# Megakernel of two gated attention/FFN layers: the output projection of the first attention in f16 high and low parts, with the orders of three engines moved around it

## The chip, the cores and the metric

The kernel runs on one core of a Trainium2 chip. The metric is device time in microseconds (us) of one execution. The engines of the core are called by their short names: PE (TensorE, matmuls), DVE (VectorE), ACT (ScalarE), POOL (GpSimd) and SP (SyncE, which here only issues DMAs). Each engine works through its own instruction stream in order; semaphores join the streams.

## The reference

The input x has 16 batches of 128 tokens with 256 features. Four sub-layers follow each other, each added to x with a gate:

```python
x = x + tanh(g_xattn[0]) * xattn0(layernorm(x), ctx, boxes, ...)   # changed here
x = x + tanh(g_ffn[0])   * bitlinear_ffn(layernorm(x), ...)
x = x + tanh(g_xattn[1]) * xattn1(layernorm(x), ctx, ...)
x = x + tanh(g_ffn[1])   * mixture_of_experts(layernorm(x), ...)

# xattn0: 16 heads of 64, 128 queries and 128 keys in each batch
q, k, v = queries @ Wq.T + bq, keys @ Wk.T + bk, values @ Wv.T + bv
a   = einsum('bhqd,bhkd->bhqk', q, k) / 8
g   = relu(sin/cos features of box differences @ Wg + bg)
mn  = softmax(log(clip(g, 1e-6)) + a)
out = einsum('bhqk,bhkd->bqhd', mn, v).reshape(b, nq, 1024)
return out @ Wo.T + bo        # 1024 -> 256, the projection that changes
```

## The kernel before, in words

Only the first attention is touched. It is a loop over the 16 batches, written out for the first and the last ones, in which every engine has a function `iteration` with a fixed order of calls. Iteration b works on three batches at once: it makes scores, gates and probabilities of batch b, projects q, k and v of batch b+1, finishes batch b-1 (probabilities times values, transposition, output projection, residual), and normalises and transposes x of batch b+2. `has_x` is false in iterations 14 and 15, `has_q` in 15, and `has_c` (or `c`) in 0.

Matmul operands that must be exact to about f32 are kept as two f16 numbers, a high part (ACT makes it with a Copy) and a low part (the f32 value less the high part, made by DVE or POOL). A product then takes three passes, written `PAIRS`: high times high, high times low, low times high. Weights are scaled by `WSC` = 64 before the split and the scale is taken out when PSUM is read. The output projection is the exception: `OT` (the transposed attention output) and `WoT` are f32, and `project_o` makes eight f32 matmuls into bank 7.

What each engine does in an iteration, in order, as far as it is spoken of below:

- PE: `row_scores` 0 (L1706), `project_qk` of r = 0, 1 (L1678), `row_scores` 1 (waits for DVE's first two `row_max`), `project_qk` of r = 2, 3, `pv` (L1766, waits for POOL's low parts of the probabilities), `project_v` 0 (L1689), `turn_o` (L1780), `project_v` 1, `turn_xn` (L1655), `project_o` (L1786), `scores` 0 (L1721, L1728), gate 0 (L1743, L1747), `scores` 1 (waits until ACT has emptied banks 0 and 1), gates 1 to 3.
- ACT: `probs_high` (L1419), `ctx_high`, `qk_high` (L1406), the two box-feature steps Abs and Ln (L1351, L1355), `v_high` 0, `take_o` (L1377, `OT` from PSUM), `v_high` 1 (L1411), `xn_high` (L1370), a one-element Exp that loads its table early (L1452), two thirds of a negation of expert weights (`half_negated`, L1383), exps 0 and 1 (`EX`, L1393), the last third, exps 2 and 3, `feature_sine` (table load and Sin L1362, Copy L1366).
- DVE: `norm` (L862), `row_max` 0, 1 (L873), `take_qk` 0, 1, `row_max` 2, 3, `take_qk` 2, 3 (L894), `take_pv` (L882, L886), `feature_floor` (L846), `take_v` (L903), `feature_turns` (L851), `xn_low` (L867), `residual` (L909, L912, waits for `project_o`), `feature_fractions` (L855, L857), `feature_distance` (eight L839), `probs` (eight L923), `bn_stats` (L1012).
- POOL: issue of an accumulating weight DMA (`half_low`, L573), `probs_low` (L560), `feature_low` (L555), `split_qk` (L546), issue of another weight DMA (`half_high`, L569), `split_v` (L551), `split_ctx` (L516), and in iterations 0 to 6 `separable`, five small operations that build tables (L521 to L530).

The expert-weight work on ACT, POOL and SP has nothing to do with the attention; it is done here for the last sub-layer.

## Time and profile before

| what | value |
|---|---|
| median of 3 runs | 1169.16 us (1166.68 to 1172.12) |
| the profiled execution: time | 1164.61 us |
| its span, first to last instruction | 1162.8 us |
| mean granted TensorE clock over the span | 0.925 |
| busy: PE, DVE, ACT, POOL | 82%, 72%, 59%, 62% |
| first attention's probabilities of batch 0 begin at | 90.69 us |
| its last residual at | 485.7 us |
| `project_o`, f32 matmuls, all 16 batches | 64.5 us |

The first attention takes about 455 us of the 1163 us span; the rest belongs to the other three sub-layers. The page's share of busy time is an average over all of them, and the order and waits inside one iteration have to be read from the timeline and from the chain of waits. The projection's row on the page counts two matmul records for each f32 matmul.

### The profile page before, as it was taken

To read this page: it belongs to the slowest core of one execution; us is meant where nothing else is said; L and a number is where in the kernel's file an instruction comes from. 1 tells how busy PE (TensorE), PEld (TensorE's weight loads), DVE (VectorE), ACT (ScalarE), POOL (GpSimd) and SP (SyncE) were. 2 spreads that over 40 slices of the span, in tenths; PEclk is the share of its full clock that TensorE was granted. 3 is DMA by queue.
4 is the path that set the end of the run, shared out by engine and by line. 5 is a ranking of instruction groups with operands and counts; after the bars stand their busy time and mean duration, and the time that the engine had idled before them with its cause. 6 is when DMAs were issued, how large, how long until landed. Compare 5 with 4: busy or idle time off the path is not lost.

```text
span 1162.8 us, 32870 instructions
## 1 busy us (share of the span) xinstructions
PE 955.3 (82%) x12178; PEld 779.8 (67%) x12178; DVE 836.2 (72%) x1947; ACT 689.7 (59%) x1338; POOL 718.9 (62%) x811
## 2 busy tenths in 40 slices
PE   0448988899999996387878559995599999999996
PEld 0336766667777764364554248873599999999995
DVE  3997888877887775657776779985566666666663
ACT  2456878888888884145425548884354545454542
POOL 2988778886677752115341539984566766666663
PEclk9888999999999997669999869995799999999998
DMA  9276667678776756330001000000555215841251
GB/s 277 72 192 142 122 129 146 150 167 183 140 149 154 154 105 148 98 130 1 1 14 41 19 2 16 26 21 19 201 142 140 32 32 140 246 142 32 32 144 16
DMA packets 52118, 119.65 MB, mean 103 GB/s; under 512 B 7617, under 2 KB 30145, under 8 KB 51633
## 3 DMA queue, kind: packets, MB, share of 16 engines
q0 software_dynamic: 14144, 35.48, 21.3%
q1 hardware_dynamic: 35520, 80.71, 20.7%
q10 hardware_dynamic: 2352, 2.10, 0.6%
q8 instruction: 66, 1.08, 0.4%
q14 instruction: 36, 0.29, 0.1%
HBM read 212.54 MB, written 37.85 MB: 215 GB/s over the span
## 4 chain that ended last, share of the span: by engine, by line
PE 51%; DVE 18%; POOL 14%; ACT 6%; issue 5%; DMA 4%; POOLq 0%; ACTq 0%; SPq 0%; DVEq 0%
PE bank L2107 17%; PE bank L2121 9%; POOL PT L560 6%; PE bank L1786 6%; PE bank L1689 3%; PE bank L1766 2%; DVE nmx L1177 2%; ACT EX L1393 2%; PE bank L1728 2%; DVE h L1063 2%; PE bank L1937 2%; PE bank L1721 1%; DVE PT L923 1%; PE bank L1780 1%; DMA gates<-in_g_ffn 1%
## 5 line engine op out<-in xcount | busy, mean ns | idle before, releaser
L1623 ACT ACTIVATE yg<-bank,bms 128x128 f32<-128x128 f32 x312 | 107.8, 364 | 106.8 <-PE bank L2107 98.9
L1296 DVE TENSOR_TENSOR hm<-hf,hm 128x256 f16<-128x256 f32 x156 | 70.3, 450 | 81.5 <-ACT hm L1630 81.5
L1291 DVE SCALAR_TENSOR_TENSOR hf<-bank,bms,yg 128x128 f32<-128x128 f32 x312 | 98.1, 345 | 33.2 <-ACT yg L1623 32.0
L2107 PE MATMUL bank<-xT,wm_even 128*128 128x128 f16 x1920 | 115.6, 221 | 1.0 <-DVE xT L1303 1.0
L2107 PEld LDWEIGHTS bank<-xT,wm_even 128*128 128x128 f16 x1920 | 111.5, 99 | 2.1 <-DVE xT L1303 1.4
L560 POOL TENSOR_TENSOR PT<-PT 128x512 f16<-128x512 f32 x64 | 72.7, 1183 | 61.4 <-ACT PT L1419 61.4
L707 POOL DMA_INDIRECT out_x<-ys,sidx x39 | 62.8, 1611 | 76.2 <-DVE ys L1310 76.2
L2107 PE MATMUL bank<-xT,wm_odd 128*128 128x128 f16 x1824 | 108.0, 219 | 1.8 <-DMA wm_odd<-expert_weights 1.8
L2107 PEld LDWEIGHTS bank<-xT,wm_odd 128*128 128x128 f16 x1824 | 104.2, 98 | 2.4 <-issue 1.9
L1630 ACT ACTIVATE hm<-hf 128x256 f16<-128x256 f32 x156 | 64.5, 414 | 63.1 <-DVE hf L1291 61.7
L619 POOL TENSOR_TENSOR h<-h 128x512 f16<-128x512 f32 x32 | 40.6, 1281 | 83.0 <-DVE h L1063 81.0
L546 POOL TENSOR_TENSOR q<-qt,q 128x512 f16<-128x512 f32 x64 | 80.0, 1299 | 0.8 <-ACT q L1406 0.7
L666 POOL TENSOR_TENSOR P<-P 128x512 f16<-128x512 f32 x64 | 72.9, 1171 | 11.4 <-ACT P L1579 11.4
L1786 PE MATMUL bank<-WoT,OT 128*128 128x256 f32 x256 | 64.5, 409 | 1.9 <-ACT OT L1377 1.9
L700 POOL DMA_INDIRECT xin<-expert_tokens,gidx x39 | 42.0, 1076 | 31.1 <-POOL b2r L722 25.5
L1786 PEld LDWEIGHTS bank<-WoT,OT 128*128 128x128 f32 x256 | 50.9, 204 | 13.3 <-ACT OT L1377 6.1
L1406 ACT ACTIVATE q<-qt 128x512 f16<-128x512 f32 x64 | 38.8, 625 | 33.8 <-DVE qt L894 33.8
L2121 PE MATMUL bank<-wm_even,hm 128*128 128x256 f16 x480 | 55.7, 273 | 2.0 <-DVE hm L1296 2.0
L717 POOL TENSOR_SCALAR gts<-xin,etf 128x1 f32<-128x1 f32 x78 | 56.3, 1091 | 0.7 <-DMA xin<-expert_tokens,gidx 0.6
L1766 PE MATMUL bank<-vv,PT 128*128 128x65 f16 x768 | 33.9, 200 | 26.4 <-POOL PT L560 15.6
L1747 PE MATMUL bank<-We,F16s 128*128 128x256 f16 x384 | 53.7, 276 | 0.0
L1689 PE MATMUL bank<-wqkv,ctx 128*128 128x512 f16 x192 | 48.1, 390 | 6.4 <-DVE qt L894 6.4
(308 smaller groups left out, 2646.7 us busy)
## 6 DMA issues: line engine op xcount, KB each, us to landing
wm_even<-expert_weights SPq DMA_DIRECT2D x60, 1024.0 KB
wm_odd<-expert_weights SPq DMA_DIRECT2D x57, 1024.0 KB
expert_weights<-in_wcat POOLq DMA_DIRECT2D x16, 768.0 KB, 7.8
wsp<-expert_weights SPq DMA_DIRECT2D x16, 768.0 KB, 4.4
wsp<-in_wcat POOLq DMA_DIRECT2D x16, 768.0 KB, 10.3
expert_weights<-wsp SPq DMA_DIRECT2D x16, 768.0 KB, 3.3
Lst<-gate_tables SPq DMA_DIRECT2D x48, 68.0 KB, 6.0
gate_tables<-Lw SPq DMA_DIRECT2D x6, 512.0 KB, 3.3
```

Source lines behind the costliest of these rows:

```text
L546: nc.gpsimd.tensor_tensor(q16[:, par, w, 1, HS * g:HS * g + HS, :], qt[:, r, :, :], hi, ALU.subtract).then_inc(s_ql, 1)
L560: nc.gpsimd.tensor_tensor(PT16[:, 1, HS * g:HS * g + HS, :], PT[:, HS * g:HS * g + HS, :], PT16[:, 0, HS * g:HS * g + HS, :], ALU.subtract ...
L666: nc.gpsimd.tensor_tensor(P116[:, b % 2, 1, HS * g:HS * g + HS, :], P1[:, b % 2, HS * g:HS * g + HS, :], P116[:, b % 2, 0, HS * g:HS * g + ...
L707: nc.gpsimd.indirect_dma_start(out=a["out"], out_offset=bass.IndirectOffsetOnAxis(ap=sidx[:, t:t + 1], axis=0), in_=ys[:, t % 2, :], in_of ...
L1291: v.scalar_tensor_tensor(hf[:, (c // 2) % 2, c % 2, :], bank[c % 4][:, MT:2 * MT], bms[:, par, FC + c:FC + c + 1], yg[:, c % 4, :], ALU.ad ...
L1296: v.tensor_tensor(hm16[:, par, 1, c - 1:c + 1, :], hf[:, q % 2, :, :], hm16[:, par, 0, c - 1:c + 1, :], ALU.subtract).then_inc(m_hl, 1)
L1623: s.activation(yg[:, c % 4, :], bank[c % 4][:, 0:MT], ACT.Gelu, bias=bms[:, par, c:c + 1]).then_inc(m_g, 1)
L1630: s.activation(hm16[:, par, 0, 2 * q:2 * q + 2, :], hf[:, q % 2, :, :], ACT.Copy).then_inc(m_hh, 1)
L1689: ins = t.matmul(bank[2 + r][:, :], ctx16[:, par, xp, kk, :], wqkv16[:, 2, wp, kk, 512 * r:512 * r + 512], start=(n == 0), stop=(n == 5))
L1786: ins = t.matmul(bank[7][:, 0:D], OT[:, ch, :], WoT[:, ch, :], start=(ch == 0), stop=(ch == CH - 1))
L2107: ins = t.matmul(bank[c % 4][:, w * MT:(w + 1) * MT], wm16[par][:, wp, col:col + P], xT16[:, par, xp * KD + kk, :], start=(n == 0), stop=( ...
L2121: ins = t.matmul(bank[5 + par][:, 0:D], hm16[:, par, xp, c, :], wm16[par][:, wp, col:col + D], start=(n == 0), stop=(n == 3 * FC - 1))
```

## The change

The projection's operands become f16 pairs, `project_o` makes 24 f16 matmuls where it made eight f32 ones, and calls are moved in the `iteration` of PE, ACT and DVE:

- Weights: `WoT` goes; the f32 weights are loaded to the place that later holds `O` and the transposed output (8 KB of a partition), ACT makes `Wo16` high once behind the first `v_high`, and DVE makes `Wo16` low in iteration 0, just before `probs` of batch 0.
- ACT: `take_o` writes f16. `xn_high` moves behind exps 0 and 1, and all three thirds of the negation stand together between `xn_high` and exps 2 and 3.
- DVE: a new `o_low` (two operations of 128x512, f16 out) stands behind `take_v`. `residual` moves from before `feature_fractions` to behind `probs`. The private semaphore of the reciprocal is replaced by the common one.
- PE: `scores` 0 moves ahead of `turn_xn` and `project_o`; behind these come `scores` 1 and then all four gates. `turn_xn` also waits for the first `o_low`, `project_o` for both.

```diff
+            def o_low(c):
+                for r in range(2):
+                    dv.wait_ge(s_oc, 2 * c + r + 1)
+                    v.tensor_tensor(OT16[:, 1, 4 * r:4 * r + 4, :], bank[6 + r][:, :].rearrange("p (c n) -> p c n", c=4),
+                                    OT16[:, 0, 4 * r:4 * r + 4, :], ALU.subtract).then_inc(s_ol, 1)
...
                 dv.wait_ge(s_op, c + 1)
-                v.tensor_tensor(otmp[:, :], bank[7][:, 0:D], bo[:, :], ALU.add).then_inc(s_opt, 1)
+                v.scalar_tensor_tensor(otmp[:, :], bank[7][:, 0:D], 1.0 / WSC, bo[:, :], ALU.mult, ALU.add).then_inc(s_opt, 1)
...
                     take_v(b + 1)
+                if has_c:
+                    o_low(b - 1)
+                if has_q:
                     feature_turns(b + 1, 1 - par)
                 if has_x:
                     xn_low(b + 2, par)
-                if has_c:
-                    residual(b - 1)
-                    dv.wait_ge(s_xu, b)
...
+                if not has_c:
+                    dv.wait_ge(s_whi, 4)
+                    v.scalar_tensor_tensor(Wo16[:, 1, :, :], woT, WSC, Wo16[:, 0, :, :], ALU.mult, ALU.subtract).then_inc(s_wlo, 1)
+                    dv.wait_ge(s_wlo, 4)
                 probs(b, not has_c)
                 if has_c:
+                    residual(b - 1)
+                    dv.wait_ge(s_xu, b)
                     v.bn_stats(...)
...
+            ac.wait_ge(s_o, 64)
+            s.activation(Wo16[:, 0, :, :], woT, ACT.Copy, scale=WSC).then_inc(s_whi, 1)
...
                 if has_q:
                     v_high(b + 1, 1 - par, (1,))
+                if has_q:
+                    s.activation(warm[:, :], nmx[:, 0:1], ACT.Exp, scale=0.0)
+                exps(b, par, (0, 1), c == 0)
                 if has_x:
                     xn_high(b + 2, par)
-                if has_q:
-                    s.activation(warm[:, :], nmx[:, 0:1], ACT.Exp, scale=0.0)
-                exps(b, par, c == 0)
+                half_negated(b, par, range(NSP))
+                exps(b, par, (2, 3), c == 0)
...
             def project_o(c):
                 pe.wait_ge(s_oc, 2 * c + 2)
-                for ch in range(CH):
-                    ins = t.matmul(bank[7][:, 0:D], OT[:, ch, :], WoT[:, ch, :], start=(ch == 0), stop=(ch == CH - 1))
+                pe.wait_ge(s_ol, 2 * c + 2)
+                n = 0
+                for (wp, op) in PAIRS:
+                    for ch in range(CH):
+                        ins = t.matmul(bank[7][:, 0:D], OT16[:, op, ch, :], Wo16[:, wp, ch, :], start=(n == 0), stop=(n == 3 * CH - 1))
+                        n += 1
...
+                scores(b, par, 0)
                 if has_x:
                     turn_xn(b + 2, (None if c == 0 else 2 * b - 1))
+                if c == 1:
+                    pe.wait_ge(s_wlo, 4)
                 if c:
                     project_o(b - 1)
-                scores(b, par, 0)
+                scores(b, par, 1)
                 gate(b, par, 0, c == 0, has_q)
-                scores(b, par, 1)
                 gate(b, par, 1, c == 0, has_q)
```

## Rows read from the trace of the kernel before

**Rows 1.** Chain of waits, early iteration (start us, us, what).

```profile
229.50 0.56 PE bank L1766 x12
...
244.52 2.12 DVE fu L839 x8
...
254.59 0.55 PE bank L1766 x12
```

**Rows 2.** Chain of waits, one late iteration.

```profile
372.62 0.56 PE bank L1766 x12
...
378.97 3.70 PE bank L1786 x16
...
391.66 4.51 POOL PT L560 x4
396.22 0.55 PE bank L1766 x12
```

**Rows 3.** Timeline, late iteration (start us, us, engine, line, tiles, [idle before]).

```profile
374.62 4.96 POOL L546 TENSOR_TENSOR q<-qt,q 128x512 f16<-128x512 f32 x4
375.59 0.73 DVE L846 TENSOR_SCALAR fu<-fu 128x1024 f32<-128x1024 f32 x1
379.21 0.63 ACT L1411 ACTIVATE vv<-vf 128x512 f16<-128x512 f32 x1 [0.31 <-DVE vf L903]
380.15 0.42 DVE L867 TENSOR_TENSOR xn<-bank,xn 128x256 f16<-128x256 f32 x1
381.54 1.99 ACT L1383 ACTIVATE wsp<-wsp 128x1024 f16<-128x1024 f16 x2
382.71 0.42 DVE L909 TENSOR_TENSOR otmp<-bank,bo 128x256 f32<-128x256 f32 x1 [2.14 <-PE bank L1786]
383.18 0.49 DVE L912 SCALAR_TENSOR_TENSOR X<-otmp,tg,X 128x256 f32<-128x256 f32 x1
383.93 1.08 ACT L1393 ACTIVATE EX<-bank 128x512 f32<-128x512 f32 x2 [0.41 <-PE bank L1728]
386.50 1.09 ACT L1393 ACTIVATE EX<-bank 128x512 f32<-128x512 f32 x2 [0.54 <-PE bank L1728]
387.68 2.74 DVE L923 SCALAR_TENSOR_TENSOR PT<-bank,EX 128x256 f32<-128x256 f32 x8
```

**Rows 4.** Timeline, early iteration.

```profile
241.45 1.10 DVE L855 TENSOR_SCALAR fks<-fu 128x1024 f32<-128x1024 f32 x1
...
249.85 1.28 DVE L873 TENSOR_REDUCE nmx<-bank 128x4 f16<-128x512 f32 x2
...
251.61 2.85 PE L1678 MATMUL bank<-ctx,wqkv 128*128 128x128 f16 x48
```

**Rows 5.** Timeline, three DVE operations beside POOL operations.

```profile
67.84 1.23 DVE L862 TENSOR_SCALAR xn<-X,mv,rstd 128x256 f32<-128x256 f32 x1
...
103.49 4.05 DVE L846 TENSOR_SCALAR fu<-fu 128x1024 f32<-128x1024 f32 x1
...
464.58 1.24 DVE L967 TENSOR_SCALAR wqkv<-wqkv,thr 128x256 f32<-128x256 f32 x1
```

**Rows 6.** Timeline, operations like the added ones.

```profile
50.03 2.28 DVE L826 SCALAR_TENSOR_TENSOR wqkv<-wst,wqkv 128x2048 f16<-128x2048 f32 x1
...
384.05 0.83 PE L1747 MATMUL bank<-We,F16s 128*128 128x256 f16 x6
...
512.09 0.69 DVE L1054 TENSOR_TENSOR xg<-bank,xg 128x512 f16<-128x512 f32 x1 [0.54 <-ACT xg L1481]
```

**Rows 7.** Iteration 0: timeline, then chain of waits.

```profile
90.69 2.07 DVE L923 SCALAR_TENSOR_TENSOR PT<-bank,EX 128x256 f32<-128x256 f32 x6
...
95.94 4.53 POOL PT L560 x4
```

**Rows 8.** Windows (us, busy of PE, PEld, DVE, ACT, POOL, then granted clock, DMA).

```profile
129.12:254.59 125.47, 113.31 (x1450) 86.16 (x1451) 103.48 (x216) 102.35 (x145) 103.90 (x96) 1.00 0.70 147
...
437.10:439.20 2.10, 0.03 (x2) 0.00 (x0) 2.03 (x5) 2.07 (x5) 0.35 (x1) 0.91 1.02 126
```

More of the change, by code:

```diff
@@ L124, in build @@
         We16 = sb("We16", [P, 2, H * NN], F16, l0)
-        WoT = sb("WoT", [P, CH, D], F32, l0)
+        Wo16 = sb("Wo16", [P, 2, CH, D], F16, l0)
         bqk = sb("bqk", [P, 2, CH], F32, l0)
@@ L881, in take_pv @@
                         dv.wait_ge(s_oe, 4 * c + f - 1)
-                    v.reciprocal(rden[:, f % 2, :].unsqueeze(2), ps[:, :, DK:DK + 1]).then_inc(s_rd, 1)
-                    dv.wait_ge(s_rd, 4 * c + f + 1)
+                    step(v.reciprocal(rden[:, f % 2, :].unsqueeze(2), ps[:, :, DK:DK + 1]))
                     if f == 0 and not first:
@@ L1022, in _ @@
             take_pv(B - 1)
+            o_low(B - 1)
             residual(B - 1)
@@ L1376, in take_o @@
                         ac.wait_ge(s_op, c)
-                    s.activation(OT[:, 4 * r:4 * r + 4, :], bank[6 + r][:, :].rearrange("p (c n) -> p c n", c=4), ACT.Copy).then_inc(s_oc, 1)
+                    s.activation(OT16[:, 0, 4 * r:4 * r + 4, :], bank[6 + r][:, :].rearrange("p (c n) -> p c n", c=4), ACT.Copy).then_inc(s_oc, 1)
             def half_negated(h, par, qs):
@@ L1383, in half_negated, with exps @@
                     s.activation(wsp[:, par, c0:c1], wsp[:, par, c0:c1], ACT.Copy, scale=-1.0).then_inc(w_ng, 1)
-            def exps(b, par, first):
-                half_negated(b, par, range(NSP - 1))
-                for g in range(4):
-                    if g == 2:
-                        half_negated(b, par, (NSP - 1,))
+            def exps(b, par, gs, first):
+                for g in gs:
                     ac.wait_ge(s_st, 4 * b + g + 1)
```

14 lines of the change are left out of this document (9 added, 5 removed).

## The prediction

> **What bounds the kernel now.** I read the chain of waits first, since only a link of it can be worth time, and looked for what repeats. In every iteration of the first attention the chain passes from `pv` (L1766) over PE and DVE to the transposed output, through `project_o`, `scores` and exps to the probabilities, then through ACT's and POOL's split of them to the next `pv`. An iteration is the distance of two `pv` starts. While POOL builds the tables (early, five full iterations) it is 254.59 - 229.50 = 25.09 us, and the last link before the probabilities is DVE's `feature_distance` [rows 1]. Later (seven iterations) it is 396.22 - 372.62 = 23.60 us, and the last link is ACT: from exps 2 and 3 at 386.50 over sine to POOL's first `probs_low` at 391.66 is 5.16 us [rows 2, 3]. `project_o`, 3.7 us, lies on both chains. From here a time with a plus is counted from the start of `pv`.
>
> **Projection, scores, exps.** Six f16 matmuls of 256 columns take 0.83 us, of which 0.27 is the length of one, so 0.11 each; 24 take 2.8 against 3.7 us [rows 2, 6]. The saving of 0.9 hardly matters, because `scores` 0 now stands ahead of it, and exps 0 and 1 no longer wait for it. ACT becomes what they wait for: `v_high` 1 ends at +7.22 (379.84), the table load and the one-element Exp take 1.39 (from 380.15, where `xn_high` has ended, to 381.54), so exps 0 and 1 begin at +8.6 instead of +11.31 [rows 3]. Then `xn_high` ends at +10.0, three thirds of the negation (two take 1.99) fill ACT to +12.75, and exps 2 and 3 start there instead of at +13.88. PE is ready: `o_low` costs 2 x 0.69 and ends at about +8, `project_o` at +10.8, `scores` 1 at +12.1, gate 3, an estimate with the gates' own spacing, at about +16.3 [rows 3, 6]. `o_low` itself costs nothing here: DVE then has `feature_turns` (about 1 us) and still waits, because `xn_low` needs `xn_high`. That is what is late next: `xn_low` at +10.0 where it stood at +7.5, a loss of 2.5 us of DVE order that eats most of the gain from taking the residual out.
>
> **Late iterations.** `xn_low` (0.40) leads to `feature_fractions` at +10.4. From there to `probs` it was 383.67 (end of L912) to 387.68, 4.0 us, so `probs` begins at +14.4 instead of +15.06 [rows 3]. Behind it `bn_stats`, `norm` and `row_max` followed, `row_max` 3.3 us after the start of `probs` (249.85 less 246.6) [rows 1, 4]. Now the residual stands in between: 383.67 - 382.71 = 0.96, with the step to the next operation 0.99 us. Nothing hides it: `row_scores` 1, `project_qk` r = 2, 3 and `pv` are queued on PE behind `row_max`. And `norm`, an operation on SBUF alone, now falls at +18.4, after POOL's first `probs_low`, which starts at 12.75 + 5.16 = +17.9 (it used to fall ahead of it). The same operation beside a POOL operation took 1.23 instead of 0.39 us, and one of its shape beside `probs_low` 1.24 [rows 5]. `norm` arrives half a microsecond into POOL's operation of 1.13, so I take 0.5 us, with bounds 0 and 0.85. `row_max` then starts at +14.4 + 3.3 + 0.99 + 0.5 = +19.2. From there to the end of `project_qk`, 249.85 to 254.46, is 4.61 us [rows 4]. `pv` starts at +23.8, and since PE and not POOL now releases it, DVE is about 0.1 later with its first part: +23.9 against 23.60. POOL would be ready at 17.9 + 4.5 = +22.4. Cost 0.3 us, seven times: +2.1.
>
> **Early iterations.** Here the DVE operations also run into POOL's table building: `feature_fractions` 1.10 instead of 0.69 [rows 3, 4]. I leave that as it is: `feature_fractions` begins at +10.4 where it stood at +11.95 (241.45 less 229.50), so `probs` at +15.6 where it was at +17.1; then 3.3 + 0.99 + 0.5 + 4.6 + 0.1 gives +25.1 against 25.09. Zero, five times. Bounds: 1.1 less each if POOL is out of the way by then.
>
> **Iteration 0.** DVE makes `Wo16` low, 2048 elements, which cost 2.28 us for `wqkv` [rows 6], right before `probs`, and `xn_low` is 2.5 late as above: `probs` from 90.69 to 95.5 [rows 7]. `probs` takes 2.7 and POOL's part follows 0.7 later, at 98.9. POOL had been free for it only at 95.94 [rows 7], so +3.0. ACT's high part (2048 elements) lies in a long idle of ACT while DVE works; it costs nothing, and about 2 us if that cover were gone. Bounds of the iteration: +1 and +6 (DVE's long operation may stand in POOL's way).
>
> **Iteration 1.** Its `feature_floor` took 4.05 us, against 0.73 elsewhere, since it came upon POOL's `split_qk` in a bad phase [rows 3, 5]. With everything before it shifted I expect the usual phase: -3.3. Bounds: 0 and -4.5 (PE's low clock behind that wait goes too).
>
> **The end.** Iteration 14 has no `xn_high` and no `norm`; exps 2 and 3 start at about +12.6 instead of +13.9 and all of it counts: -1.2. In iteration 15 the residual only changes its place in DVE's own chain: 0. Behind the loop `o_low` (0.69) is exposed and the f16 passes gain nothing at half clock: +0.7. The removed reciprocal semaphore replaces one wait by another, 0.
>
> **Sum.** 2.1 + 0 + 3.0 - 3.3 - 1.2 + 0.7 = +1.3 us on the profiled execution's 1164.6 us (span 1162.8), so 1165.9. The median of the runs shown lies 4.5 us above that execution; the forecast for the median is 1170.5, rounded to 1171.
>
> **A rule on the port.** The trace shows DVE operations that last longer by about a POOL operation, and one by 3.3 us [rows 5]. The Trainium skill, "SBUF — State Buffer", section "Who interferes with whom", says that a DVE operation in a two-port mode or with two SBUF inputs and a GpSimd operation exclude each other, the second being blocked for the whole of the first. By that rule alone `norm` waits for the rest of POOL's operation, which is the bound of the late term already; but it also speaks against the change in a second place, the first rival.
>
> **Rivals.**
>
> *`feature_floor` meets `split_qk` (slower).* POOL's `split_qk` starts 6.56 us after its `probs_low` (391.66 - 23.60 = 368.06, to 374.62) [rows 2, 3]. It now starts at +17.9 + 6.6 = +24.5, 0.6 to 0.7 after the next `pv` instead of 2.0. Its four operations of 1.13 then begin near +0.7, 1.8, 2.95 and 4.1, and `feature_floor` asks at +3.0 to +3.1. Before, it asked just ahead of an operation and won. Behind one it waits some 0.9 us; ACT has 0.31 us of idle to absorb it [rows 3], so 0.5 us x 12 = +6: 1177. It decides if `feature_floor` comes later than POOL's third operation. Repeated misses as in iteration 1 (until the fourth ends, 1.7 us x 12) give +20: 1191.
>
> *PE's clock drops (slower).* It was 1.00 through the early iterations. After PE stood nearly idle for 2.1 us in iteration 14 the window already shows 0.91 [rows 8]. In early iterations PE now waits for `row_max` some 2.4 us (it ends the first half of `project_qk` at +19.5), in late ones 1.3. At the half clock `project_qk` (2.85, [rows 4]) costs 1.5 to 2.9 more, five times: 1179 to 1185.
>
> *`norm` does not collide and early DVE work is freed (faster).* If POOL's `probs_low` lets `norm` through, 0.5 x 12 = 6 us go: 1165. If also the early iterations lose POOL's tables from DVE's way (1.1 x 5), 1160. For it: POOL's stream now runs earlier against DVE. Against it: the 1.23 and 1.24 us of [rows 5]. It decides when `norm` costs 0.4 us in most iterations.
>
> *The gain of moving the scores stays whole (faster).* This needs `xn_low` not to be what `feature_fractions` waits for; the order of ACT excludes it.
>
> **How the numbers follow.** A measurement of this kernel can tell about 0.5%, 6 us, from no change. The computed case: 0.34, 1167 to 1175 by the bounds of its terms. `feature_floor`: 0.20. The clock, alone or with it: 0.15. Repeated misses: 0.04. The faster cases: 0.27, of which 0.24 end below 1163.3. Above 1175 lie nearly all of the slower cases. So faster 0.25, same 0.39, slower 0.36, and the range that leaves out the two ends is 1160 to 1184; the computed case alone would be 1166 to 1176.
>
> **What would show it.** Exps 0 and 1 at +8.6 and 2 and 3 at +12.7; DVE idle before `xn_low`, released by `xn_high`; L909 and L912 behind L923; L862 at 0.9 to 1.2 us instead of 0.39; PE idle before L1706, released by `nmx`, and no wait of `pv` on POOL; `probs` of batch 0 at 95 to 96 us; L846 of iteration 1 at 0.7. I am wrong if L862 stays at 0.39 (then faster), if L846 is at 1.5 or more in most iterations, or if the granted clock between 100 and 260 us is below 0.98 (then slower), or if `probs` of batch 0 comes at 93 or earlier or after 98 us.

## The result, and the profile after

| | before | after |
|---|---|---|
| median of 4 runs each, same chip | 1169.65 us (1166.68 to 1172.12) | 1187.06 us (1184.98 to 1188.65) |
| the profiled execution, its span | 1164.61, 1162.8 us | 1187.89, 1185.9 us |
| mean granted clock over the span | 0.925 | 0.917 |
| probabilities of batch 0 begin at | 90.69 us | 97.66 us |
| last residual at | 485.7 us | 501.0 us |

The ratio is 1.0149, with a 95% interval of 1.0119 to 1.0179: the change costs 17.4 us, where the forecast was a level 1171 with a range up to 1184. The first attention accounts for 501.0 - 485.7 = 15.3 us of it. Behind the attention the two profiled executions differ by 7.8 us more, but the one of before lay 5 us below its own median; the rest, some 2 us, is less than the interval can tell. A rare execution of any kernel ran at a low clock over its whole span (one of the kernel before 1638.78 us at 0.56, one of H below 1589.93 us at 0.58); no ratio here counts one. What follows splits the 15.3.

The distance between two starts of `probs` gives the iterations (the same instruction, L923 before and L931 after):

| stretch | before | after | difference, sum |
|---|---|---|---|
| `probs` of batch 0 | 90.69 | 97.66 | +7.0 |
| iteration 0 to 1 | 29.89 | 25.20 | -4.7 |
| five periods up to batch 6 | 25.60, then 25.1 | 26.78, 26.74, 26.78, 25.65, 26.78 | +6.7 |
| batch 6 to 7 | 23.10 | 25.26 | +2.2 |
| six periods up to batch 13 | 23.60 | 24.29 | +4.1 |
| 13 to 14, 14 to 15 | 23.60, 26.08 | 22.47, 25.94 | -1.3 |
| `probs` 15 to last residual | 24.74 | 26.03 | +1.3 |

A late iteration, the chain of waits of the changed kernel (start us, us, what), against [rows 2]:

```profile
378.11 2.62 DVE PT L931 x8
...
381.10 0.49 DVE X L920
...
381.97 0.93 DVE xn L865
382.89 1.21 DVE nmx L876 x2
...
384.64 2.80 PE bank L1695 x48
...
390.45 1.70 DVE fu L849
...
394.26 1.30 DVE OO L912 x2
...
395.70 2.78 PE bank L1806 x24
...
400.58 1.83 DVE fu L842 x7
402.40 1.62 DVE PT L931 x5
```

ACT and POOL have nearly left the chain. It goes through DVE and PE: residual, `norm`, `row_max`, `project_qk`, then `feature_floor` (L849), `o_low` (L912), `project_o` (L1806). The timeline of the same iteration, against [rows 3] (`pv` starts at 387.26):

```profile
384.24 0.40 PE L1723 MATMUL bank<-q 64*128 64x128 f16 x8 [1.49 <-DVE nmx L876]
...
388.19 4.97 POOL L549 TENSOR_TENSOR q<-qt,q 128x512 f16<-128x512 f32 x4
390.45 1.69 DVE L849 TENSOR_SCALAR fu<-fu 128x1024 f32<-128x1024 f32 x1
392.17 1.06 ACT L1370 ACTIVATE fu<-fu 128x1024 f32<-128x1024 f32 x1 [1.10 <-DVE fu L849]
395.47 1.52 DVE L854 TENSOR_SCALAR fu<-fu,cst 128x1024 f32<-128x1024 f32 x1
396.66 1.07 ACT L1405 ACTIVATE EX<-bank 128x512 f32<-128x512 f32 x2
398.03 0.42 DVE L870 TENSOR_TENSOR xn<-bank,xn 128x256 f16<-128x256 f32 x1 [1.04 <-ACT xn L1385]
400.72 1.09 ACT L1405 ACTIVATE EX<-bank 128x512 f32<-128x512 f32 x2
402.28 2.73 DVE L931 SCALAR_TENSOR_TENSOR PT<-bank,EX 128x256 f32<-128x256 f32 x8
```

POOL's `split_qk` starts 0.93 us after `pv` where it started 2.0 after; `feature_floor` asks at +3.19, 0.02 us after its third operation has begun, and lasts 1.69 instead of 0.73. ACT, which waited 0.48 us for it before, waits 1.10; its other idle time, 0.31 us before the second `v_high`, is gone. Everything behind is late by the rest: exps 0 and 1 at +9.40 (forecast +8.6), 2 and 3 at +13.5 (+12.7), `xn_low` at +10.8 (+10.0), `probs` at +15.0 (+14.4).

An early iteration, timeline, against [rows 4]:

```profile
177.27 2.84 PE L1695 MATMUL bank<-xn,wqkv 128*128 128x128 f16 x48 [0.19 <-DVE PT L931]
180.34 0.82 DVE L865 TENSOR_SCALAR xn<-X,mv,rstd 128x256 f32<-128x256 f32 x1
181.09 1.27 DVE L876 TENSOR_REDUCE nmx<-bank 128x4 f16<-128x512 f32 x2
182.51 0.40 PE L1723 MATMUL bank<-q 64*128 64x128 f16 x8 [2.40 <-DVE nmx L876]
182.84 4.48 PE L1695 MATMUL bank<-ctx,wqkv 128*128 128x128 f16 x48
```

The second half of `project_qk`, 48 matmuls, lasts 4.48 us behind an idle time of PE of 2.40; the first half, also 48, lasts 2.84. The clock is low for part of the 4.48 us only: 31 of these matmuls start 107 ns after one another, most of the others 56. The windows (last columns: granted clock, DMA share, GB/s) show the clock below full speed there, and at full speed in the late stretch:

```profile
140.00:260.00 120.00, 103.34 (x1359) 80.93 (x1358) 103.24 (x207) 93.59 (x136) 93.09 (x86) 0.96 0.64 133
280.00:420.00 140.00, 123.17 (x1724) 95.58 (x1723) 125.48 (x263) 114.97 (x166) 97.59 (x83) 1.00 0.71 145
```

Iteration 0, against [rows 7]:

```profile
84.69 0.42 DVE L870 TENSOR_TENSOR xn<-bank,xn 128x256 f16<-128x256 f32 x1 [2.99 <-ACT xn L1385]
85.03 3.43 DVE L858 TENSOR_SCALAR fks<-fu 128x1024 f32<-128x1024 f32 x1
...
95.35 2.28 DVE L1020 SCALAR_TENSOR_TENSOR Wo<-OO,Wo 128x2048 f16<-128x2048 f32 x1
97.66 2.74 DVE L931 SCALAR_TENSOR_TENSOR PT<-bank,EX 128x256 f32<-128x256 f32 x8
...
113.87 3.87 DVE L854 TENSOR_SCALAR fu<-fu,cst 128x1024 f32<-128x1024 f32 x1
```

`xn_low` is 2.5 us late (82.21 before), the weights' low part takes its 2.28, and `feature_fractions` L858, which now starts inside POOL's block (from 83.92 on), lasts 3.43 instead of 0.68. J below shows that the 2.5 us alone are not to blame for the meeting. Iteration 1 has a long collision again, now `feature_turns` (L854) with 3.87 instead of `feature_floor` with 4.05 [rows 5].

### The profile page after: what moved, and what is told of

Read it like the earlier page. It is cut to its first block, busy times and chain, and to the rows that moved or that the text cites. A ratio compares the mean times of both kernels' runs of the same rounds, so it can differ in the third digit from the quotient of the medians.

```text
span 1185.9 us, 33162 instructions
## 1 busy us (share of the span) xinstructions
PE 950.5 (80%) x12306; PEld 778.2 (66%) x12306; DVE 870.3 (73%) x1980; ACT 683.0 (58%) x1339; POOL 722.9 (61%) x811
## 4 chain that ended last, share of the span: by engine, by line
PE 44%; DVE 28%; ACT 9%; issue 7%; POOL 6%; DMA 5%; SPq 0%; ACTq 0%; DVEq 0%; POOLq 0%
PE bank L2130 16%; PE bank L2144 8%; PE bank L1695 5%; DVE PT L931 3%; DVE fu L842 3%; DVE fu L849 2%; PE bank L1806 2%; DVE h L1078 2%; DVE nmx L1192 2%; PE bank L1960 2%; DVE nmx L876 1%; PE bank L1783 1%; ACT wsp L1398 1%; PE bank L1922 1%; DMA gates<-in_g_ffn 1%
## 5 line engine op out<-in xcount | busy, mean ns | idle before, releaser
L1311 DVE TENSOR_TENSOR hm<-hf,hm 128x256 f16<-128x256 f32 x156 | 66.7, 428 | 100.2 <-ACT hm L1646 97.0
L2130 PE MATMUL bank<-xT,wm_even 128*128 128x128 f16 x1920 | 118.0, 221 | 3.3 <-DVE hf L1306 2.2
L1306 DVE SCALAR_TENSOR_TENSOR hf<-bank,bms,yg 128x128 f32<-128x128 f32 x312 | 98.5, 346 | 27.0 <-ACT yg L1639 25.5
L549 POOL TENSOR_TENSOR q<-qt,q 128x512 f16<-128x512 f32 x64 | 77.4, 1238 | 1.2 <-ACT q L1418 1.1
L1695 PE MATMUL bank<-xn,wqkv 128*128 128x128 f16 x768 | 49.0, 227 | 10.5 <-DVE PT L931 9.2
L1695 PEld LDWEIGHTS bank<-xn,wqkv 128*128 128x128 f16 x768 | 46.6, 102 | 12.5 <-issue 11.7
L1695 PE MATMUL bank<-ctx,wqkv 128*128 128x128 f16 x768 | 54.7, 241 | 0.0
L896 DVE SCALAR_TENSOR_TENSOR qt<-bank,bqk 128x512 f32<-128x512 f32 x64 | 42.3, 681 | 15.5 <-PE bank L1695 15.5
```

The source lines that it names most:

```text
L549: nc.gpsimd.tensor_tensor(q16[:, par, w, 1, HS * g:HS * g + HS, :], qt[:, r, :, :], hi, ALU.subtract).then_inc(s_ql, 1)
L1306: v.scalar_tensor_tensor(hf[:, (c // 2) % 2, c % 2, :], bank[c % 4][:, MT:2 * MT], bms[:, par, FC + c:FC + c + 1], yg[:, c % 4, :], ALU.ad ...
L1311: v.tensor_tensor(hm16[:, par, 1, c - 1:c + 1, :], hf[:, q % 2, :, :], hm16[:, par, 0, c - 1:c + 1, :], ALU.subtract).then_inc(m_hl, 1)
L1695: ins = t.matmul(bank[2 + r][:, c * N:(c + 1) * N], wqkv16[:, w, wp, kk, col:col + P], src[:, par, xp, kk, :], start=(n == 0), stop=(n == 5))
L2130: ins = t.matmul(bank[c % 4][:, w * MT:(w + 1) * MT], wm16[par][:, wp, col:col + P], xT16[:, par, xp * KD + kk, :], start=(n == 0), stop=( ...
```

## The experiments

Eighteen kernels ran. Ratios are to the kernel before, run on the same chip in turn. Its median there was 1171 to 1173 us for A to L and 1164.5 for M to R, so the times of different groups are compared by their ratios.

| kernel | median us | ratio, 95% interval |
|---|---|---|
| the change | 1187.06 | 1.0149 (1.0119 to 1.0179) |
| A old orders | 1180.76 | 1.0082 (1.0063 to 1.0101) |
| B residual back | 1179.00 | 1.0072 (1.0045 to 1.0100) |
| C residual split | 1175.99 | 1.0032 (1.0014 to 1.0050) |
| D filling | 1180.14 | 1.0064 (1.0047 to 1.0080) |
| E turns first | 1200.15 | 1.0246 (1.0199 to 1.0292) |
| F weights' low part early | 1181.22 | 1.0088 (1.0056 to 1.0119) |
| G C + E + F | 1170.03 | 0.9988 (0.9957 to 1.0019) |
| H G + filling | 1201.12 | 1.0247 (1.0179 to 1.0315) |
| I POOL waits | 1202.29 | 1.0273 (1.0239 to 1.0307) |
| J `xn_high` back | 1184.66 | 1.0115 (1.0080 to 1.0150) |
| K G, X's update later | 1168.79 | 0.9984 (0.9963 to 1.0004) |
| L K + J | 1173.06 | 1.0022 (1.0006 to 1.0037) |
| M `norm` first | 1169.63 | 1.0036 (1.0018 to 1.0054) |
| N without `o_low` | 1176.28 | 1.0095 (1.0058 to 1.0132) |
| O G, iteration 1 mended | 1161.43 | 0.9977 (0.9961 to 0.9994) |
| P H again | 1191.40 | 1.0231 (1.0181 to 1.0281) |
| Q M + F | 1165.56 | 1.0016 (1.0004 to 1.0028) |
| R M + F + filling | 1163.73 | 0.9998 (0.9978 to 1.0017) |

**A and B: are the new orders the cost?** A keeps the f16 projection and puts all old orders back; B puts the residual alone back before `feature_fractions`.

```diff
                 if has_x:
                     xn_low(b + 2, par)
+                if has_c:
+                    residual(b - 1)
+                    dv.wait_ge(s_xu, b)
...
                 probs(b, not has_c)
                 if has_c:
-                    residual(b - 1)
-                    dv.wait_ge(s_xu, b)
```

> The f16 projection alone: the orders of PE, ACT and the place of the residual are those of the kernel before; o_low stands behind take_v, Wo16 low before the first probs. Theory (the loss comes from DVE operations that meet POOL and from PE's clock, both brought about by the new orders): project_o starts 1.6 us later, behind the second o_low, and is 0.9 us shorter, so each iteration is 0.7 us longer than before (25.8 early, 24.3 late), plus 2.3 us in iteration 0 and 0.7 behind the loop: about 1180 us. feature_floor stays at 0.74, norm at 0.39, the clock of the early iterations at 1.00. Rival (the projection itself, with its added DVE work, is the loss): 1187 us with collisions as in the changed kernel.

> The changed kernel with the residual back between xn_low and feature_fractions. Theory: probs starts 1.1 us later in the iteration, but row_max is free of residual and collision (1.6 us), POOL again releases pv, so the phase of feature_floor is the old one (0.74 instead of 1.5) and PE's gap is short, with clock 1.00: late iterations 23.5 to 24.1 us instead of 24.28, early ones about 25.2 instead of 26.5: about 1178 us. Rival (the residual's place is no cause): 1.0 us more in each iteration, 1200 us.

Measured 1180.8 and 1179.0, as expected, but in part by luck. In both, `norm` (0.41) and the late `feature_floor` (0.74) are free of collisions, and the time lost is still 6 to 10 us. `feature_turns` took the collision over: it lasts 3.19 us in the late iterations, 3.9 to 4.3 in early ones, where it was about 1 before. The same in C, below. Putting one call back moves the victim along; this was in none of my rivals.

Whether it costs anything is told by the chain of waits. In B and C, and in A's early iterations (26.03 us, 25.8 expected), the chain passes through `feature_turns`. In A's late ones (24.22, 24.3 expected) it does not; it passes through `o_low` and `project_o`, and the loss of 0.62 is what A's theory named: `project_o` starts 1.55 us later behind `o_low` and is 0.92 shorter. A's chain, late:

```profile
341.48 1.21 DVE OO L912 x2
...
342.82 2.78 PE bank L1808 x24
```

So of the change's 1.49% the new orders make 0.67, some 8 us, and 0.82 are there with the f16 projection in the old orders.

**C and D: the residual off the path, and the clock.** C updates X and does `bn_stats` one iteration later, in DVE's wait, and leaves only the reading of the bank behind `probs`. D puts five 512-column matmuls whose product is not used into PE's wait.

```diff
                 probs(b, not has_c)
                 if has_c:
-                    residual(b - 1)
-                    dv.wait_ge(s_xu, b)
-                    v.bn_stats(...)
+                    residual_first(b - 1)      # bank 7 to otmp; C
...
+                if has_c and not first:
+                    finish(b - 2)              # otmp into X, bn_stats; before xn_low; C
...
+                if c and has_q:                # PE, before row_scores 1; D
+                    pe.wait_ge(s_xh, b + 2)
+                    pe.wait_ge(s_xl, b + 2)
+                    for _ in range(5):
+                        t.matmul(bank[6][:, :], ident16[:, :], wqkv16[:, 0, 0, 0, 0:512], start=True, stop=True)
```

> The changed kernel with only the first residual operation (bank 7 to otmp) behind probs; the update of X and bn_stats run one iteration later, in DVE's wait for xn_high. Theory: norm starts ahead of POOL's probs_low and costs 0.39, row_max comes 1.4 us earlier, PE's gap and the low clock go, POOL releases pv and feature_floor no longer meets split_qk: late iterations 22.6 to 23.2 us, early ones about 24.5, in all 15 to 22 us less, 1165 to 1172 us. Rival (the losses are not in this link): within 3 us of 1187.

> The changed kernel with five f16 matmuls of 512 columns into the free bank 6, ahead of the second row_scores, where PE waits; they add work whose result nobody reads. Theory (the clock is a cause of its own in the early iterations): the granted clock of the early iterations goes from 0.95 to 1.00, project_qk behind the gap from 4.1 to 2.85 us, early iterations from 26.5 to about 25.2, late ones stay at 24.28: about 1180 us. Rival (the low clock only fills a wait that something else sets): no change, 1187, with the clock at 1.00.

C: 1176.0. The timeline of a late iteration:

```profile
386.83 1.28 DVE L912 TENSOR_TENSOR OO<-bank,OO 128x512 f16<-128x512 f32 x2
388.03 3.19 DVE L854 TENSOR_SCALAR fu<-fu,cst 128x1024 f32<-128x1024 f32 x1
391.15 0.47 DVE L922 SCALAR_TENSOR_TENSOR X<-otmp,tg,X 128x256 f32<-128x256 f32 x1
...
387.83 2.21 POOL L554 TENSOR_TENSOR vv<-vf,vv 128x512 f16<-128x512 f32 x2
389.99 0.68 POOL L519 TENSOR_TENSOR ctx<-ctxf,ctx 128x256 f16<-128x256 f32 x1
```

`feature_turns` asks 0.2 us after `split_v` has begun, gets in at neither of the two boundaries that follow, and ends 0.5 us after POOL's block does. The two DVE operations of `o_low` had pushed it there: in G, with `feature_turns` ahead of them, it lasts 1.03.

D: 1180.1, by the medians 7 us and by the ratios 10 us below the change. The granted clock between 140 and 260 us is 1.00, the second half of `project_qk` 2.85, the early iterations are 25.67 (25.2 expected) instead of mostly 26.78. `norm`, `feature_floor` and `feature_turns` (0.83, 1.69, 1.52) last as long as in the change's one early period at full clock. In its slow periods `feature_floor` lasts only 1.16 to 1.31, for it asks later within POOL's operation. So of the 1.63 us more for the matmuls 1.1 reach the period: 26.78 against the one early period of the change at 25.65, and 26.61 against 25.51 in N below, where the same projection is seen at 4.48 and at 2.85. The last residual is at 495.5 instead of 501.0, although iteration 1 lost 1.5 in D. So the low clock alone is worth 6 to 10 us of the 17.4, by the last residual or by the ratios.

**E and F: one edit each.** E puts `feature_turns` ahead of `o_low`; F makes the weights' low part in DVE's idle 2.99 us of iteration 0.

```diff
                     take_v(b + 1)
+                    feature_turns(b + 1, 1 - par)      # E
                 if has_c:
                     o_low(b - 1)
-                if has_q:
-                    feature_turns(b + 1, 1 - par)
+                if not has_c:                          # F: the four lines of Wo16 low
+                    dv.wait_ge(s_whi, 4)
...
                 if has_x:
                     xn_low(b + 2, par)
```

> The changed kernel with one order of VectorE put back: feature_turns stands ahead of o_low again (as it stood before the change), o_low behind it. Theory (the second half of VectorE's loss is that o_low pushes feature_turns, 1024 elements on SBUF alone, into POOL's split_qk): feature_turns goes from 1.52 late and 1.30 to 1.46 early to 1.03, so -0.3 to -0.5 in each of 13 iterations, 1181 to 1184 us; feature_floor stays at 1.69 late. Rival (the block of POOL operations costs the same wherever VectorE meets it first, and ACT's xn_high is what xn_low waits for anyway): nothing, 1186 to 1188 us, with VectorE's idle time before xn_low longer by the same 0.3 to 0.5.

> The changed kernel with the low part of Wo16 made earlier in iteration 0: in VectorE's idle 2.99 us before xn_low instead of right before probs. Theory (the 2.28 us lie bare on the chain of iteration 0): probs of batch 0 goes from 97.66 to 95.4, and since POOL was free for it at 95.94 before, 1.7 to 2.3 us less: 1184.8 to 1185.4 us. Rival 1 (half a dozen later collisions depend on the phase that this sets; iteration 1's feature_turns took 3.87 us): up to 3 us less again, 1182, or as much more. Rival 2: POOL or ACT is late in iteration 0 anyway: 1187.

E: 1200.2, by the ratios 11 and by the medians 13 us above the change. The theory was wrong, and so was the rival. PE's timeline, late:

```profile
351.23 0.41 PE L1671 MATMUL bank<-ident,xn 128*128 128x128 f32 x2 [1.71 <-DVE OO L912]
351.83 4.45 PE L1805 MATMUL bank<-Wo,OO 128*128 128x256 f16 x24 [0.19 <-DVE OO L912]
```

`feature_floor` (1.69) and `feature_turns` (1.54) now both stand before `o_low`; PE waits 1.71 for it and runs `project_o` mostly at half clock, 4.45 us instead of 2.78, in two of three late iterations. These take 26.4 to 26.7 us, the third 25.25. Where `o_low` stands decides how long PE is idle.

F: 1181.2, 6 to 7 us below the change. `probs` of batch 0 begins at 93.81, 3.85 earlier than in the change, of which 2.28 are the operation and most of the rest is `feature_fractions`, 1.41 instead of 3.43. The periods behind it are nearly the same, and the last residual is 4.9 us earlier. So iteration 0's loss was real, and nothing hid it.

**G, K, O: the whole repair.** G is C + E + F. K moves X's update and `bn_stats` behind `feature_fractions` and has `o_low` ahead of `feature_turns` in iteration 1 alone. O is G with this last edit only.

```diff
+                if has_q and not first:
+                    feature_turns(b + 1, 1 - par)
                 if has_c:
                     o_low(b - 1)
+                if first:
+                    feature_turns(b + 1, 1 - par)
...
                 if has_q:
                     feature_fractions(b + 1, 1 - par)
+                if has_c and not first:        # K; in G and O before xn_low
+                    finish(b - 2)
```

> The split residual of the earlier run (X's update and bn_stats one iteration later, in VectorE's wait), with feature_turns ahead of o_low and the low part of Wo16 made early. In the run with the split residual alone, 1176.0 us, a late iteration was 23.91 us and feature_turns 3.19 us. Theory (what is left of the loss is that operation's meeting with split_qk): feature_turns 1.03, xn_low then waits for xn_high until 390.3 where it stood at 392.0, so 1.6 us less in each late iteration and about 2 in each early one: 1152 to 1160 us, below the kernel before. Rival (whatever VectorE does there first waits for the block of POOL operations; the order only changes the name of the victim): feature_turns or feature_floor at 1.7 to 3.2, 1170 to 1176 us.

> The earlier run with the split residual and feature_turns first (1170.0 us), with two edits more: X's update and bn_stats stand behind feature_fractions, where POOL is idle late, and in iteration 1 alone o_low stands ahead of feature_turns. Theory: X's update lasted 2.13 us late and 3.27 early by its meeting with split_v, it goes to 0.48, but VectorE then waits for xn_high; the sum 1.4 idle, 0.33, 1.86, 0.85, 2.14 puts probs 0.2 us earlier late and up to 1 earlier in early iterations; iteration 1 goes from 28.7 to some 25.5 (o_low no longer waits behind feature_turns' 5.09 us, so PE's wait of 5.26 us and its low clock go). 1158 to 1166 us. Rival (the later phase makes feature_turns or feature_floor the next victim): 1168 to 1175.

> The run with 1170.0 us (residual split, feature_turns first, low part of Wo16 early), with o_low ahead of feature_turns in iteration 1 alone. Theory (the 28.7 us of iteration 1 there are o_low's wait behind feature_turns, PE's idle 5.26 and its low clock after it): that iteration goes to about 25.2 as in the run with X's update moved, the other periods stay at 25.46 and 23.50: 1166 to 1168 us. Rival (the phase set by iteration 1 changes the others): late iterations of 23.9 or early ones of 26, 1170 to 1176.

G: 1170.0, level with before, not 1152 to 1160: `feature_turns` (1.03), `feature_floor` (0.74) and `norm` (0.41) are all free, a late iteration is 23.50, an early one 25.46, but X's update is the next victim. O shows it, DVE's timeline and POOL's:

```profile
375.14 0.74 DVE L849 TENSOR_SCALAR fu<-fu 128x1024 f32<-128x1024 f32 x1
...
378.65 1.04 DVE L854 TENSOR_SCALAR fu<-fu,cst 128x1024 f32<-128x1024 f32 x1
379.61 1.27 DVE L912 TENSOR_TENSOR OO<-bank,OO 128x512 f16<-128x512 f32 x2
380.81 2.14 DVE L922 SCALAR_TENSOR_TENSOR X<-otmp,tg,X 128x256 f32<-128x256 f32 x1
...
379.82 2.21 POOL L554 TENSOR_TENSOR vv<-vf,vv 128x512 f16<-128x512 f32 x2
381.98 0.67 POOL L519 TENSOR_TENSOR ctx<-ctxf,ctx 128x256 f16<-128x256 f32 x1
```

K frees X's update (0.48 late) and gains next to nothing: DVE waits 1.31 or 2.01 for `xn_high` in its place, and the earlier `probs` puts every second `feature_floor` at 1.68; the late periods alternate between 23.17 and 23.88. O mends iteration 1 (25.02 instead of 28.73) and is, at 0.9977, the fastest of all, 3 us below the kernel before, a difference that its interval (0.9961 to 0.9994) just shows.

**H and P: filling on top of G** (the lines of D).

> The run before this one, with five filling matmuls of 512 columns in PE's wait before row_scores 1 (their product is not used). Theory (the granted clock of 0.96 in the early iterations comes from that wait and costs PE's projections): clock 1.00 between 140 and 260 us, and up to 0.8 us less in each of five early iterations, 0 to 4 us below the run before this one. Rival (with the residual split, PE's wait is short enough and the clock is 1.00 there already, so that the filling only delays row_scores): equal or up to 3 us longer.

> The same kernel as the one with the filling matmuls on top of the split residual, whose first profile is not usable. Theory: its filling waits for xn_low and then delays row_scores 1, project_qk and pv by 1.0 to 1.3 us in each of 13 iterations, since PE had only 0.35 us of idle there, and feature_floor leaves its good phase: late iterations of 24.5 to 25.5, clock 1.00, 1185 to 1200 us. Rival: the granted clock fell (below 0.95 in the stretch from 280 to 420 us).

H's median is 1201, but its four comparable executions scatter from 1183 to 1203 us, and its profile is of the fifth, of 1590 us, which says nothing here. P repeats the kernel with 1189 and 1193 us. P's profile shows the picture of E: the filling delays `row_scores` 1, `feature_floor` falls to 1.70 and `feature_turns` to 1.55, PE waits 1.72 for `o_low` and `project_o` takes 4.45 in three of the five iterations between 280 and 420 us. The clock is 0.93 over 140 to 260 us and 0.96 over 280 to 420, neither the 1.00 of the theory nor the rival's below 0.95 in that stretch: what fills one wait has opened another.

**I and J: two waits by themselves.**

```diff
                 if has_q:
+                    gp.wait_ge(s_fv, 4 * b + 5)        # I: POOL, feature_floor done
                     split_qk(b + 1, 1 - par)
...
+                if has_x:                              # J: ACT, ahead of the Exp
+                    xn_high(b + 2, par)
                 if has_q:
                     s.activation(warm[:, :], nmx[:, 0:1], ACT.Exp, scale=0.0)
                 exps(b, par, (0, 1), c == 0)
-                if has_x:
-                    xn_high(b + 2, par)
```

> The changed kernel with one wait more on POOL: split_qk begins only when VectorE's feature_floor is done. Theory (feature_floor's 1.69 us late are 0.95 of waiting behind POOL, and all that follows on ACT and VectorE inherits them): feature_floor 0.74; split_qk starts about 3.8 us after pv instead of 0.9 and ends at about +8.8, so feature_turns, at +7.2, now meets it: a gain of 0.9 if feature_turns gets in between its operations, a loss of 1 to 1.5 if it has to wait for split_qk's end. With the multi-operation wait seen elsewhere (3.2 to 4.3 us) the late iterations are 24.3 to 25.5 and the time is 1187 to 1200 us; without it 23.4 and 1175 us. Rival (POOL becomes the bound since its split_v ends late): pv late, 1195 or more with VectorE waiting for pv.

> The changed kernel with ACT's xn_high ahead of the one-element Exp and exps 0 and 1 again, as before the change; the rest of ACT's new order stays. Theory (VectorE's 1.04 us of idle before xn_low are ACT's lateness with xn_high, and lie on the chain through feature_fractions and feature_distance to probs): xn_low about 1 us earlier, late iteration 23.4 instead of 24.28, and 9 to 12 us in all: 1175 to 1178. Rival (exps 2 and 3 end the chain to probs, 0.4 later than now since all of ACT's work moves by xn_high): -0.2 to +0.4 per iteration, 1184 to 1192 us.

I: 1202.3, 2 us above the forecast's worst branch. `feature_floor` is free (0.68) and `feature_turns` nearly (1.12), yet `feature_fractions` now meets the late `split_v` (357.59 to 359.81). The timelines of DVE and POOL:

```profile
351.64 0.68 DVE L850 TENSOR_SCALAR fu<-fu 128x1024 f32<-128x1024 f32 x1
...
359.04 1.96 DVE L859 TENSOR_SCALAR fks<-fu 128x1024 f32<-128x1024 f32 x1
...
352.40 4.51 POOL L549 TENSOR_TENSOR q<-qt,q 128x512 f16<-128x512 f32 x4 [2.98 <-DVE fu L850]
```

The clock is 0.94 early and 0.96 late (0.96 and 1.00 in the change): PE now waits 2.40 us for `row_max` in late iterations too. J: 1184.7, so the rival was right. `xn_low` has no wait any more, but `probs` waits 0.94 us for PE's gates, which wait for exps. The first line below is of iteration 0:

```profile
83.06 5.17 DVE L860 TENSOR_TENSOR fu<-fu,fks 128x1024 f32<-128x1024 f32 x1
...
345.93 0.41 DVE L870 TENSOR_TENSOR xn<-bank,xn 128x256 f16<-128x256 f32 x1
...
351.33 1.75 DVE L931 SCALAR_TENSOR_TENSOR PT<-bank,EX 128x256 f32<-128x256 f32 x5 [0.94 <-PE bank L1764]
```

A late iteration became 24.70 (`norm` lasts 1.31 in it). In iteration 0 the edit takes away the 2.5 us by which `xn_low` was late, and L858 is free (0.69), but `probs` begins at 96.31, only 1.35 us earlier: the second operation of `feature_fractions`, L860, is the victim with 5.17 us instead of 1.23. **L**, the same edit on top of K, also lost (24.02 against a mean of 23.53, with L858 at 1.57 instead of 0.68).

> The run before this one, with ACT's xn_high ahead of the one-element Exp and exps 0 and 1. Theory (with X's update out of the way, xn_high is what VectorE waits for): 1.0 to 1.4 us less idle before xn_low, a late iteration 22.2 to 22.5 instead of 23.3, 1145 to 1155 us. Rival (project_o and scores 1, and behind them exps 2 and 3, end at the same time as feature_distance: in the run with 1170.0 us exps 2 and 3 ended 1.5 us before probs): the gain stops at 0.3 to 0.9 us per iteration, 1150 to 1160; or less, if the phase against POOL's block turns bad, 1170.

**M and N: which of the collisions counts.** M does `norm` directly behind `probs` and the residual after it. N leaves `o_low` out: the low part of the attention output is not computed, and the pass that used it takes the high part again.

```diff
                 probs(b, not has_c)
+                if has_x and not last:
+                    norm(b + 3, b + 3)
                 if has_c:
                     residual(b - 1)
```

> The changed kernel with VectorE's norm directly behind probs and the residual behind norm (the order of the change is probs, residual, bn_stats, norm); nothing else differs. Theory: norm then runs before POOL's probs_low begins (0.41 us as in the run with the split residual, not 0.94), row_max 0.5 us earlier in each of 12 iterations, and since the path from row_max over row_scores 1 and project_qk to pv has no other cover, 6 us less: 1180 to 1182. Rival 1 (the residual, an operation of VectorE with X in SBUF, now meets probs_low in norm's place): 1186 to 1188. Rival 2 (feature_floor asks half a microsecond earlier against POOL's split_qk and waits as much longer): 1186 to 1188 with feature_floor at 1.2 or at more than 1.69.

> The changed kernel without o_low on VectorE: the low part of the transposed attention output is left out of the computation, and the pass that used it repeats the high part, so PE's 24 matmuls stay. Theory of the forecast (o_low costs nothing in the loop, since VectorE waits for xn_high behind it): late iterations as before at 24.2 to 24.3, the end 0.7 less: 1184 to 1187 us. Rival (o_low delays PE's project_o and scores 1 and the clock falls in the early iterations): the early iterations go from 26.7 to 25.7, 5 to 7 us less: 1179 to 1182. Second rival (feature_turns comes earlier and meets split_qk for longer): slower, 1190 or more, with feature_turns above 2.

M: ratio 1.0036, 1.1% or 13 us below the change, for one short call moved ahead of three others. `norm` lasts 0.40 and the residual meets nothing either (0.48). A late iteration is 23.46, a gain of 0.83, more than the 0.54 of `norm` alone, since `split_qk` starts 1.65 us after `pv` instead of 0.93: `feature_floor` asks 0.46 us into its second operation, not 0.02 into its third, and lasts 1.24 instead of 1.69. `feature_turns` is worse (2.58), and it costs nothing: it ends when `xn_high` is ready.

```profile
348.94 0.40 DVE L865 TENSOR_SCALAR xn<-X,mv,rstd 128x256 f32<-128x256 f32 x1
...
358.19 1.24 DVE L849 TENSOR_SCALAR fu<-fu 128x1024 f32<-128x1024 f32 x1
...
362.90 2.57 DVE L854 TENSOR_SCALAR fu<-fu,cst 128x1024 f32<-128x1024 f32 x1
365.39 0.41 DVE L870 TENSOR_TENSOR xn<-bank,xn 128x256 f16<-128x256 f32 x1
```

PE's early wait is 1.97 in M; behind three of these waits the 48 matmuls take 4.41 to 4.48 us, behind three others 2.85. PE, early, one of the latter:

```profile
180.08 0.40 PE L1727 MATMUL bank<-q 64*128 64x128 f16 x8 [1.97 <-DVE nmx L876]
180.41 2.85 PE L1699 MATMUL bank<-ctx,wqkv 128*128 128x128 f16 x48
```

N: ratio 1.0095, 6 us below the change, but not by either mechanism that I had named. The late iterations are 24.29, as forecast: there `o_low` is free. The early ones are 26.6 or 25.5, hardly changed. Most of the gain lies in no stretch of the attention that I could single out: the last residual is at 498.8 instead of 501.0. What the other 4 us are stays open (N's profiled execution lay 2.8 us above its own median, and the intervals of both ratios are about 4 us wide to each side).

**Q and R: do the parts add up?** Q is M + F, R is Q with D's filling.

> Norm ahead of the residual, and the low part of Wo16 in VectorE's idle before xn_low in iteration 0. Theory (the parts add up): probs of batch 0 about 3.5 us earlier as in the run with that edit alone, so ratio to before 1.0036 - 0.003 = 1.0005, 1165 us on a chip where before takes 1164.6. Rival (another phase in the early iterations): 26.3 us in all of them instead of a mix with 25.4, 1.002 to 1.004.

> The run before this one with five filling matmuls of 512 columns before row_scores 1. Theory (PE's idle of 1.97 to 2.4 us there in the early iterations is what lowers the clock of project_qk behind it): clock 1.00 between 140 and 260 us, project_qk r = 2, 3 at 2.85 us in all, early iterations of 25.3 to 25.5, 3 to 5 us below the run before this one: ratio 0.997. In the late iterations PE's idle is 0.99 and the filling of 1.24 us has to wait for xn_low only, so at most 0.3 us each are lost, 2 us, which would leave 1 to 3. Rival (as in the run where filling stood on the split residual, the delay puts feature_floor into its bad phase): 1.01 or more.

1.0016 and 0.9998. In Q the parts do not quite add up: `probs` of batch 0 begins at 95.18, 2.0 us earlier than in M and not 3.5, since L858 lasts 3.68 there, against 1.41 and 1.42 in F and R with the same edit. In R the clock between 140 and 260 us is 1.00, PE's wait there is 0.89, all six early periods are 25.3 to 25.5 and the late ones 23.3 to 23.5. The last residual stands at 482.0, 3.7 us before that of the kernel before:

```profile
140.00:260.00 120.00, 106.12 (x1422) 80.18 (x1422) 112.09 (x219) 93.93 (x134) 99.07 (x88) 1.00 0.68 140
280.00:420.00 140.00, 134.36 (x1817) 101.96 (x1816) 126.86 (x266) 120.14 (x172) 97.02 (x84) 1.00 0.73 150
```

Three repairs, each aimed at one named loss, take back 1.0149 to 0.9998. The filling's own share on top of Q, 1.8 us by the medians, is not clear of the intervals; in D it was.

## Why the prediction was wrong

The terms of the sum run from one start of `pv` to the next. Counted so, and not from `probs` to `probs` as in the table above, the 15.3 us stand against the 1.3 of the sum like this:

| term of the sum | forecast | measured |
|---|---|---|
| iteration 0 | +3.0 | +5.3 |
| iteration 1 | -3.3 | -0.9 |
| early, five times | 0 | +7.3 |
| late, seven times | +2.1 | +3.4 |
| iterations 14 and 15 | -1.2 | -1.2 |
| behind the loop | +0.7 | +1.4 |

**Late iterations (+0.3 forecast, +0.69 measured).** The path behind `probs` was right: no wait of `pv` on POOL, `row_max` 4.82 us after `probs` (forecast 4.8), 4.60 from there to the end of `project_qk` (4.61), `norm` at 0.94 instead of 0.89. The step that failed stands in the first rival: I worked out that `feature_floor` would ask at +3.0 to +3.1 and `split_qk`'s third operation begin at +2.95, wrote that it loses if it comes later, and left it out of the sum. It waited 0.95, ACT's idle absorbed 0.3, and `probs` was at +15.0 instead of +14.4. From there to the next `pv` it was 9.26 us where the sum had 9.5, so 0.4 of the 0.6 is left. Five of the seven lose 0.68 to 0.73, the first 0.15 and the last nothing.

**Early iterations ("zero, five times"; +6.7 measured, and +2.2 for the next).** The sum named a wait of PE of some 2.4 us, and a price of 1.5 to 2.9 for the half clock; measured were 2.40 and 4.48 - 2.85 = 1.63, of which 1.1 count, in five of the six periods up to batch 7 (in two of them the clock falls at `row_scores` 1 already, and the 48 matmuls take 4.18 and 4.12). The other 0.55 is seen in the one period at full clock, 25.65 against 25.10: `probs` at +16.5 instead of +15.6, behind the same `feature_floor` of 1.69 as late, and 9.2 us from there to `pv` where the sum had 9.5. The rival had mechanism and size right, the choice was wrong, and this is the largest step that failed: I kept full clock although [rows 8] showed the clock at 0.91 behind a nearly idle stretch of 2.1 us. D takes this cause away from the change and shows it; R does the same to Q. It and the floor's collision, two rivals with 0.15 and 0.20, came together. The 0.15 was for the clock "alone or with it", but its price of 1179 to 1185 held the clock alone, and the range ended at 1184.

**Iteration 0 (`probs` +4.8 forecast, +7.0 measured; `pv` +3.0 forecast, +5.3 measured).** The 2.5 us of `xn_high` and the 2.28 us of the weights were right. The step that failed is that `feature_fractions` was taken as free on the way: it ran into POOL's block, +2.75. F took 3.85 of the 7.0 back. J shows that POOL's block catches the other half of `feature_fractions` without the 2.5 us.

**Iteration 1 (-3.3 forecast, -0.9 measured).** Its long collision did not go, as the term wanted. `feature_floor` still lasts 1.55, and the rest moved to `feature_turns` (3.87), where part of it is covered. What went is `project_o` at half clock behind PE's wait (5.41 us before, 2.78 after), and what came is the half clock in `project_qk` (4.18 instead of 2.85). The -4.7 between the starts of `probs` look better only because losses of both iterations lie behind `probs`.

**Iterations 14 and 15 and the end.** Right in mechanism, the end 0.7 too small.

**`o_low` "costs nothing here".** Shown for the late iterations by N. But in A's late iterations it lies on the chain of waits with its 1.2 us, A to C show that its 1.2 us shift `feature_turns` into POOL's `split_v`, and E and P that PE waits for it; it is free only in the order in which the change has it.

**The gain that did come.** `project_o` fell from 3.70 to 2.78 us, and exps 0 and 1 no longer wait for it. But it starts at +8.4 instead of +6.35, behind `feature_floor` and `o_low`, so that the late `probs` is at +15.02 where it was at +15.06, and all of the 0.69 lies behind it, in the residual and `norm`, which `pv` now waits for.

**The rule on the port.** The Trainium skill, "SBUF — State Buffer", section "Who interferes with whom", has the second operation blocked for the length of the first. `norm` (+0.54) and `feature_floor` (+0.95) agree with it, since POOL's operations last 1.12 to 1.24 us. The 3.19 us of `feature_turns` in C don't: the POOL operation under way and the two behind it passed ahead of it.

## What to carry to other kernels

When the critical engine shares something with another, a change of order has to be costed by the phase of each operation against the other engine's block, and a case in which 0.1 us decides belongs in the sum with half its price, not beside it. Look for the short operation that everything waits for (`norm` here) and put it ahead of longer work that nobody waits for; one such move, with the phases that it changed, was worth 13 us. And where a reordering makes PE wait longer, price the matmuls behind the wait at half clock as the likely case once the kernel's own trace shows a drop at such a wait.

## What the runs showed that I had not expected

- A DVE operation of 1024 elements on SBUF alone does not always get in when POOL's current operation ends. `feature_turns` took 3.19 us beside `split_v` and `split_ctx` in C, 3.71 to 3.72 beside POOL's table building in R, 5.09 in iteration 1 of G, and 1.03 when free. `feature_floor`, of the same size, waited for one boundary (1.69) in the late iterations of the change and for several in iteration 1 of the kernel before (4.05). `feature_fractions`' second operation, a tensor_tensor with both inputs in SBUF, took 5.17 and 5.15 in iteration 0 of J and A, 1.23 when free. Why one boundary lets it in and another does not is open.
- The eight `feature_distance` operations of 128 elements get in one by one, each between two operations of POOL's table building: 5.38 us for eight in iteration 0, 2.14 when free.
- PE idle for 1.97 us was followed by 48 matmuls in 2.85 us or in 4.48 us in one and the same execution (M), and so was PE idle for 2.40 us (N, and the change itself); after 1.58 us (E) they took 2.85. In E's late iterations an idle time of 1.71, with one of 1.08 or 1.09 some 12 us ahead of it, was followed by `project_o` at 4.45 in two of three and at 2.78 in the third.
